# An attention half step waits for its column banks ahead of its rows, on one core of a Trainium2 chip

## The reference

```
Q, K, V = heads(norm(x))                      # biased projections
scores  = Q K^T / 4 + lambda * (tanh(Q) J) tanh(K)^T
scores  = where(causal, scores, -inf)
probs   = softmax(scores)                     # by rows
out     = probs V, then a projection, + x
x       = x + shared expert + sum of two weighted experts
```

## Time and profile before

| | us |
|---|---|
| median of three runs | 2475.45 |
| the profiled execution, its own time | 2476.85 |
| span of its profile | 2475.1 |
| TensorE busy in the span | 2222.3 (90%) |
| VectorE busy | 1266.8 (51%) |
| ScalarE busy | 1029.4 (42%) |
| GpSimd busy | 622.7 (25%) |

### The profile page before, as it was taken

How to read it: one execution, slowest core, us unless ns; L and a number is a source line. 1 busy time by engine, 2 the same in 40 slices (tenths; PEclk the granted TensorE clock), 3 DMA queues, 4 the chain that set the end, 5 groups by cost and what they waited for, 6 DMA issues and landing times. The chain is left out here.

```text
span 2475.1 us, 49744 instructions
## 1 busy us (share of the span) xinstructions
PE 2222.3 (90%) x14878; PEld 1413.3 (57%) x14879; DVE 1266.8 (51%) x3832; ACT 1029.4 (42%) x1752; POOL 622.7 (25%) x1000
## 2 busy tenths in 40 slices
PE   3899989999899999999998298879999999997885
PEld 1345445454445454554454187657777777776674
DVE  4555545555455554555451665434444444443775
ACT  1344444444453444444442132245555555553321
POOL 0012111111111111111121088656100000001786
PEclk9798999999998999999986599989999999999997
DMA  6211222122221222122200554343211111112785
GB/s 208 71 39 42 71 66 80 36 69 71 66 63 42 71 65 80 41 63 71 56 25 26 197 172 162 133 146 130 78 55 55 55 55 54 54 53 100 241 261 186
DMA packets 149366, 223.41 MB, mean 90 GB/s; under 512 B 18512, under 2 KB 104528, under 8 KB 149200
## 3 DMA queue, kind: packets, MB, share of 16 engines
q1 hardware_dynamic: 130000, 173.72, 22.8%
q0 software_dynamic: 15744, 46.16, 5.7%
q10 hardware_dynamic: 3456, 1.34, 0.2%
HBM read 110.26 MB, written 77.33 MB: 76 GB/s over the span
## 5 line engine op out<-in xcount | busy, mean ns | idle before, releaser
L599 DVE CUSTOM_DVE_ANT_0 ps_rows<-ps_rows,maskrow 128x512 f32<-128x512 f32 (+3 forms) x1024 | 480.9, 516 | 430.6 <-PE ps_rows L445 428.0
L546 ACT ACTIVATE probs<-ps_cols 128x1024 f32<-128x1024 f32 (+3 forms) x512 | 360.2, 704 | 531.4 <-PE ps_cols L463 523.2
L445 PE MATMUL ps_rows<-ks,qs 32*128 32x512 f32 (+3 forms) x2048 | 432.1, 507 | 30.8 <-issue 20.9
L459 PE MATMUL ps_cols<-qs,ks 32*128 32x512 f32 (+3 forms) x2048 | 440.0, 507 | 16.0 <-ACT probs L546 16.0
L700 POOL TENSOR_TENSOR pace<-eps 1x1 f32<-1x1 f32 x256 | 46.8, 183 | 1091.1 <-ACT probs L546 1091.1
L463 PE MATMUL ps_cols<-mT,ones_r 32*128 32x512 f32 (+3 forms) x1024 | 298.8, 577 | 0.0
L445 PEld LDWEIGHTS ps_rows<-ks,qs 32*128 32x128 f32 x2048 | 161.5, 192 | 192.3 <-issue 150.2
L1607 DVE TENSOR_TENSOR h_lo<-ps_h,h_hi 128x512 fp32r<-128x512 f32 x135 | 93.3, 691 | 254.4 <-ACT h_hi L1579 254.4
L459 PEld LDWEIGHTS ps_cols<-qs,ks 32*128 32x128 f32 x2048 | 160.0, 191 | 68.8 <-ACT probs L546 61.4
L476 PE MATMUL ps_o<-probs,vt 128*32 128x512 f32 (+3 forms) x2048 | 197.3, 458 | 0.0
L1573 ACT ACTIVATE sg_e<-ps_ge 128x512 f32<-128x512 f32 x135 | 80.7, 598 | 266.6 <-PE ps_ge L1499 266.6
(11 more groups left out here) (200 smaller groups left out, 3885.1 us busy)
## 6 DMA issues: line engine op xcount, KB each, us to landing
xs_d<-zrows SPq DMA_DIRECT2D x45, 384.0 KB, 3.2
xr<-xs_d SPq DMA_DIRECT2D x135, 128.0 KB, 2.0
yo_d<-y_e SPq DMA_DIRECT2D x135, 128.0 KB, 1.7
xn<-in_L_attn_x_dram SPq DMA_DIRECT2D x16, 512.0 KB, 4.3
ks<-k_lin SPq DMA_DIRECT2D x64, 128.0 KB, 2.4
ks<-k_tan SPq DMA_DIRECT2D x64, 128.0 KB, 2.3
qs<-q_lin SPq DMA_DIRECT2D x64, 128.0 KB, 2.6
qs<-q_mix SPq DMA_DIRECT2D x64, 128.0 KB, 2.3
```

Source lines behind the costliest of these rows:

```text
L445: mm = nc.tensor.matmul(ps_rows[s][:, e, 0:(it + 1) * P], qs[at:at + STRIP, d.par, g, it * P:(it + 1) * P], ks[at:at + STRIP, d.par, g, 0: ...
L459: nc.tensor.matmul(ps_cols[:, e, jt * P:S], ks[at:at + STRIP, b.par, g, jt * P:(jt + 1) * P], qs[at:at + STRIP, b.par, g, jt * P:S], start ...
L546: nc.scalar.activation(probs[:, n % 2, 2 * (1 - s):2 * (1 - s) + 2, jt * P:S], ps_cols[:, :, jt * P:S], ACT.Exp).then_inc(exp_done, 1)
L599: a = nc.vector.tensor_tensor_reduce(out=bank, in0=bank, in1=maskrow[:, (TT - 1 - it) * P:S], scale=1.0, scalar=LOWEST, op0=ALU.add, op1=A ...
```

## The change

The wait for `exp_done` moves out of `cols` into a new function `banks_free`, which is called ahead of `rows` in each half step. The values waited for stay the same.

```diff
+        def banks_free(b, n, s):
+
+            if b.at_least(0) and b.at_most(NB - 1) and not (b.fixed and b.off == 0 and n == 0 and s == 0):
+                pe.wait_ge(exp_done, (b.v * STEPS + n) * 2 + s)
+
         def rows(b, n, s):
...
@@ cols @@
             if s == 0 and jt == 0:
                 pe.wait_ge(taken["mt"], count("mt", g, b))
-            if not (b.fixed and b.off == 0 and n == 0 and s == 0):
-
-                pe.wait_ge(exp_done, (b.v * STEPS + n) * 2 + s)
             for e in range(2):
...
@@ batch @@
+                banks_free(b, n, 0)
                 rows(b, n, 0)
                 if att:
                     cols(b, n, 0)
                 piece(b, n, 0)
+                banks_free(b, n, 1)
                 rows(b, n, 1)
                 if att:
                     cols(b, n, 1)
```

## The result

| | before | after |
|---|---|---|
| median, us | 2468.62 (20 runs, 2455.01 to 2480.79) | 2484.34 (20 runs, 2474.46 to 2495.88) |
| profiled execution, us | 2476.85 | 2489.01 |
| granted clock, mean of the span | 0.936 | 0.932 |

The ratio of after to before is 1.0062, with a 95% interval from 1.0046 to 1.0078. That is 15.3 us slower (11.4 to 19.3). The forecast was 18.5 us over a median of 2475.45, a ratio of 1.0075. The granted clocks of the table are those of the two profiled executions; over all 20 runs of the changed kernel the mean was 0.936.

The account below looks back on a forecast made before the run. Bound by a chain of half steps: in some TensorE is late, in others it waits for the exponential. Loop 15.7, just behind an exponential 1.7, outside 0.8: 18.2 us, 2495.0 profiled, 2494 median; range 2479 to 2508.

Parts of the forecast that it names:

- The lead of the rows: In waiting half steps, rows moving back to the columns' start were said to cost the columns nothing: 0.
- Rival D: In waiting half steps, the late columns are what costs; removing the rows' lead would give back 80 us; chance 0.01.
- The wait's place: In the loop the wait moves from a matmul to a register instruction: 0.07 us more for each waiting half step.
- Rival B: A register wait is no dearer here, since 0.13 us came after VectorE, 0.06 after ScalarE; 2479, no change; chance 0.12.
- The order: Rows' weight loads go ahead of the columns': 0.015 us for each waiting half step, 0.02 in the loop.
- The longer lags just after the sequencer was held: After a stop in the loop, columns may come further behind the rows than 0.015 us; 0.05 kept for the range.
- 174 x (0.07 + 0.02): Loop's sum: 174 waiting half steps, each paying 0.07 us for the wait's place and 0.02 for order, 15.7 us.
- the 24 half steps just behind an exponential: Two per batch start their rows a little after an exponential; in the loop 0.07 us each, 1.7 us together.
- The 56 outside the loop: Waiting half steps in the four batches outside the loop, wait still on a matmul: 0.015 us each, 0.8 us.
- rival A: TensorE idle instead of busy lowers the clock at three batch starts, 3 us each: 27 us in all, 2503; chance 0.18.
- Rival C: Rows and columns together keep the clock up over batch ends; 0.02 of granted clock would bring 18 us; chance 0.07.

Follow-up runs that it names:

- e2: Kernel before, with the rows' matmuls issued between the two pairs of column matmuls, so the columns go first and carry the exp_done wait; ratio 0.9911.
- e3: Kernel before, with a second, always fulfilled wait in the loop that pushes the columns' real wait onto a register instruction; ratio 0.9984.
- e1: Changed kernel, with the two waits ahead of the rows swapped in the loop, so exp_done stays on the rows' matmul; ratio to before 1.0012.
- e4: Changed kernel, with one more always fulfilled wait in the loop, so two register instructions stand between exponential and rows; ratio to before 1.0101.
- c1: Kernel before, run once more unedited against itself; ratio 0.9970.
- d3: e3 run once more, unedited; ratio to the kernel before 0.9987.
- d1: Changed kernel, run once more unedited on the chip of the comparisons; ratio to the kernel before 1.0049.
- d2: e1 run once more, unedited; ratio to the kernel before 0.9987.
- c2: e2 run once more, unedited; ratio to the kernel before 0.9963.
- c3: Kernel before, with all batches written out and no loop in the attention; ratio 0.9833.

## Why the prediction came out

**The lead of the rows, 0: right.** e2 has no lead and the old stretch. Rival D, that the late columns cost, falls with the same run, and with the 1.28 us from columns to next job in the timeline after.

**The wait's place, 0.07 us: right.** 0.122 us from release to load against 0.052. e3 shows that it is the place by itself, since the order is the old one; e1 that with the wait on the matmul it is gone; e4 that a second register instruction costs 0.092 us more. The forecast's value came from a single wait of a later stage, read to 0.01 us, so that it was met so closely is partly luck. Rival B said that the 0.13 of the earlier trace rows might be VectorE's. It falls: the exponentials are ScalarE's, and the value is the same. The rule of the Trainium skill that a sequencer's instruction waits before the next is fetched, while TensorE's waits in a queue behind it ("Perfetto Trace Analysis", Per-engine timelines), agrees with 0.122 and 0.052.

**The order, 0.015 to 0.02: right.** The columns' loads stand 0.018 behind the rows' in the loop and 0.013 outside. The longer lags just after the sequencer was held did not come in the waiting half steps.

**The size, 18.2 us: too high by about 2.** The term that was mis-sized is "174 x (0.07 + 0.02)". Twelve of the 174 keep their wait on the matmul and pay 0.012, the others pay 0.088, and the 24 half steps just behind an exponential pay 0.055 and not 0.07: 162 x 0.088 + 12 x 0.012 + 24 x 0.055 = 15.7 us for the loop, where the forecast had 17.4 and the stretches and batch ends give some 16. The 56 outside the loop pay 0.012 each, 0.7 instead of 0.8. The whole-time result, 15.3 us (11.4 to 19.3), can't tell 16.4 from 18.2. The list of instructions on each engine shows those twelve ahead of any run; I had looked at it only at step 7.

**The clock, rival A: not borne out.** The sign that the prediction asked for, a mean granted clock of the loop away from 0.96 by 0.01 or more, didn't come: it is 0.96 before and after. In 14 traces with twelve stretches each, the clock fell inside a stretch once, in e4, although TensorE stands idle for up to 0.9 us there. The oscillation that the Trainium skill describes for a TensorE that waits between its groups of matmuls ("TensorE: Matmul & The Clock Gate", HAM oscillation) isn't seen at these short spells; it is seen at the loop's jumps, where TensorE is idle for about 4 us and the clock fell every time. Around the batch ends, single traces seem to say that the changed order draws more of it. Traces in which the rows lead had 78.5, 51.2, 54.6 and 54.6 us low in the loop (before, c1, e3, d3), a mean of 60; those where rows and columns go together behind the wait had 81.9, 71.7, 88.7, 92.2 and 68.3 (after, d1, e1, d2, e4), a mean of 81. But e2 and c2, whose rows have lost their lead too, had 61.4 and 58.0, which speaks against the lost cover as the cause. And over all runs the granted clock doesn't follow: d1 has 0.9276 beside 0.9264 of the kernel before, d2 the same as it, e4 0.9280 beside 0.9274, and only e1 less, 0.9243. At equal clock the changed kernel's cost is 18 us, so it is not the clock's. Rival C, that the order wins the clock back, has nothing for it: 0.0012 in d1, where it asked for 0.02.

**What stays open.** d3's runs had a granted clock 0.010 above the kernel before, e3's 0.0055. That is why their times equal it in spite of a loop that takes 956.8 and 956.6 us, 14 more than c1's. Two sets of the kernel before itself (c1 and the runs beside it) differ by 0.0045, so e3's gain could be chance; d3's is more than that, and why the old order with the wait on a register instruction should have it, no run here shows.

**The best version** is the kernel before with its batches written out, at 0.9833 (0.9789 to 0.9878) of the time before. It hardly touches the disputed wait, which is on the matmul in both; it takes away the jumps and the low clock behind them. With the loop kept, the kernel before beats the changed one.

## What to carry to other kernels

Ask of every wait on the critical path which instruction will carry it, not only ahead of which line it is written. A second wait or a computed value in front of a matmul can move the first to the sequencer, and that is paid each time (0.07 us here); with the wait that ends last directly ahead of the matmul it was not paid (e1). Work that fills a wait is cover, and moving it cost nothing here (e2), as long as the operand that is released last still starts at the same time. Where the clock's draw is larger than the effect, measure between two fixed instructions in a stretch at full clock, hold the whole-time ratio against a second run set of the same kernel, and set each run's time beside its granted clock: two kernels can have equal times because one costs more and drew a better clock.

## What the runs showed of the hardware

- A matmul whose wait is its own starts its weight load 0.052 us after the last instruction of the awaited engine ends. With a register instruction holding the wait, it is 0.122, and 0.092 more for each further one in between (e4).
- At a jump at the end of a round of the loop TensorE is idle for about 4 us (4.1 to 4.3 in the kernel before), and with that and the lower clock that comes behind it the batch end is 18 to 22 us long instead of 12.6. Without the jump c3 took 12.49 us at the same place. I had not expected that six rounds of a loop cost more than the change studied.
- From its step 2 to its step 15 the last batch took 50.4 us in one execution without any low clock (e2) and 62.5 with 29.5 us of it (e3), in kernels with nearly the same instructions.
- A microsecond at the low clock costs less than half of itself here: a batch end without a jump took 17.62 us with 13.7 us low and 12.59 with none, in the same trace of the kernel before, 0.37 us for each. Over 2530 us, 0.001 of granted clock is 5.1 us at the low clock, which makes the 1.9 us of the slope (an estimate).
